# Second norm of a language-model tower: the variance computed one sequence ahead, the values kept by VectorE, one whole tanh two sequences behind, and the next turn between the halves of the second product

## The reference, cut to what matters

```python
h = h + _L0_ffn_ref(_layernorm(h, axis=-1), ...)
h = h + _L1_attn_ref(_layernorm(h, axis=-1), ...)

def _layernorm(x, axis=-1, eps=1e-05):
    m = jnp.mean(x, axis=axis, keepdims=True)
    v = jnp.var(x, axis=axis, keepdims=True)
    return (x - m) / jnp.sqrt(v + eps)

def _L1_attn_ref(x, Wk1, bk1, Wk2, bk2, Wq1, bq1, Wq2, bq2, Wv, bv, ln_w, ln_b, Wo, bo):
    def encode(W1, b1, W2, b2):
        h = jax.nn.gelu(x @ W1 + b1, approximate=False)
        return jnp.tanh(h @ W2 + b2)
    key_phase = encode(Wk1, bk1, Wk2, bk2) * freq * jnp.pi
    query_phase = encode(Wq1, bq1, Wq2, bq2) * freq * jnp.pi
    key_phasor = jnp.cos(key_phase) + 1j * jnp.sin(key_phase)
    V = (x @ Wv + bv).astype(jnp.complex64)
    ...
```

## Time and profile before

| | |
|---|---|
| median of 3 runs | 1166.69 us (1165.56 to 1167.3) |
| profiled execution, its own time | 1167.59 us |
| its span | 1165.8 us |
| busy share of the span | TensorE 95%, VectorE 60%, ScalarE 68%, GpSimd 12% |
| chain that ended last, by engine | TensorE 85%, VectorE 6%, ScalarE 4%, GpSimd 2% |
| the stage of the change | about 872 to 930 us |

### The profile page before, as it was taken

How to read it: one execution, slowest core, us unless ns; L and a number is a source line. 1 busy time by engine, 2 the same in 40 slices (tenths; PEclk the granted TensorE clock), 3 DMA queues, 4 the chain that set the end, 5 groups by cost and what they waited for, 6 DMA issues and landing times.

```text
span 1165.8 us, 62466 instructions
## 1 busy us (share of the span) xinstructions
PE 1103.2 (95%) x26872; PEld 931.7 (80%) x26872; DVE 694.8 (60%) x3130; ACT 795.1 (68%) x4592; POOL 143.2 (12%) x220
## 2 busy tenths in 40 slices
PE   3799999999999999999999999999898699899998
PEld 2699999999999999999999999999544388622322
DVE  7565455555555555555555554444466669899985
ACT  1467677777777777777777777666568888556654
POOL 4200000000000000000000000000104212412110
PEclk9555555555555555555555555555699989999999
DMA  4000000000000000000000000000000000447675
GB/s 142 8 9 9 9 14 9 10 9 9 10 13 9 9 9 10 14 9 9 10 4 4 5 5 4 4 4 4 2 1 1 1 1 1 148 157 291 210 267 173
DMA packets 30545, 47.20 MB, mean 40 GB/s; under 512 B 12274, under 2 KB 21563, under 8 KB 30268
## 3 DMA queue, kind: packets, MB, share of 16 engines
q1 hardware_dynamic: 30268, 43.21, 11.0%
HBM read 40.84 MB, written 2.36 MB: 37 GB/s over the span
## 4 chain that ended last, share of the span: by engine, by line
PE 85%; DVE 6%; ACT 4%; POOL 2%; issue 1%; DMA 1%; SPq 1%; DVEq 0%; ACTq 0%; POOLq 0%
PE bank L657 44%; PE bank L753 7%; PE bank L1383 6%; PE bank L1676 5%; PE bank L736 5%; PE bank L427 4%; PE bank L526 3%; PE bank L731 2%; PE bank L748 1%; PE bank L1581 1%; PE bank L412 1%; POOL stat L1024 1%; PE bank L1416 1%; PE bank L447 1%; DMA bsum<-in_bov 1%
## 5 line engine op out<-in xcount | busy, mean ns | idle before, releaser
L657 PE MATMUL bank<-space,whh_hi 128*128 128x8 f16 x16384 | 609.9, 169 | 7.4 <-DVE space L784 4.2
L657 PEld LDWEIGHTS bank<-space,whh_hi 128*128 128x128 f16 x16384 | 528.7, 105 | 25.5 <-DVE space L784 7.4
L784 DVE TENSOR_TENSOR space<-h_f,space 128x16 f16<-128x16 f32 x2048 | 290.6, 175 | 381.5 <-ACT h_f L765 379.9
L765 ACT ACTIVATE h_f<-bank 128x16 f32<-128x16 f32 x2048 | 300.0, 184 | 230.0 <-PE bank L657 222.5
L771 ACT ACTIVATE space<-bank 128x16 f16<-128x16 f32 x2048 | 299.0, 184 | 1.1 <-PE bank L657 1.1
L657 PE MATMUL bank<-space,whh_lo 128*128 128x32 f16 (+1 forms) x2096 | 145.0, 190 | 0.0
L753 PE MATMUL bank<-space,wih_hi 128*128 128x32 f16 x2048 | 137.1, 188 | 0.0
L427 PE MATMUL bank<-onehot,tab 128*128 128x128 f16 x448 | 116.7, 266 | 0.5 <-DVE prepare_cur L477 0.5
L736 PE MATMUL bank<-xr,wih_hi 128*128 128x32 f16 x512 | 109.8, 214 | 0.0
L1266 ACT ACTIVATE gel<-bank,ebias 128x1024 f32<-128x1024 f32 x64 | 71.3, 1114 | 56.1 <-PE bank L1383 50.6
L731 PE MATMUL bank<-ones,bias 128*128 128x32 bf16 x512 | 102.8, 201 | 0.0
(11 more groups left out here) (288 smaller groups left out, 1559.4 us busy)
## 6 DMA issues: line engine op xcount, KB each, us to landing
space<-weights_kept SPq DMA_DIRECT2D x64, 512.0 KB, 7.9
space<-in_x SPq DMA_DIRECT2D x28, 129.0 KB, 3.1
out<-res SPq DMA_DIRECT2D x8, 256.0 KB, 9.7
space<-in_wrec SPq DMA_DIRECT2D x1, 768.0 KB, 4.0
space<-in_wx SPq DMA_DIRECT2D x1, 740.5 KB, 8.8
brec<-in_brec SPq DMA_DIRECT2D x1, 260.0 KB
ew<-in_ew SPq DMA_DIRECT2D x1, 256.0 KB, 4.1
weights_kept<-wturned SPq DMA_DIRECT2D x8, 32.0 KB, 1.8
```

The source lines that it names most:

```text
L657: mm = pe.matmul(own[:, m, :], w[:, k, m * P:(m + 1) * P], steps(h, k), start=False, stop=False, skip_group_check=True)
L765: act.activation(h_f[layer][:, s % 2, :, :], own, ACT.Tanh, scale=scale[layer]).then_inc(s_h[layer], 1)
L784: dve.tensor_tensor(h[layer][:, :, s % RINGS[layer], 1, :], h_f[layer][:, s % 2, :, :], h[layer][:, :, s % RINGS[layer], 0, :], ALU.subtra ...
```

## The change

The variance of sequence b+1 is computed before the normalising product of b, with its own three columns of `stat` for even and odd sequences (`rstd_row`). The values are kept by VectorE (`values_kept`, one sequence behind) instead of ScalarE. The tanh is one instruction over 1024 columns, runs two sequences behind, and its product goes to banks 2 and 3 or 6 and 7 in turn (`phase_bank`). The second product is split: its first half, the turn of the next sequence, its second half. The last sequence is turned and copied whole. A wait for all tanhs stands before the bias product in bank 6.

The hunk that only removes the semaphores `s_half` and `s_half_kept` is left out.

```diff
@@ -914,6 +913,8 @@
         FF_B1, KQ_B1, KQ_B2, LN_W, LN_B, QUARTER, WR_B, GRID, FF_B2, TURN, BACK = 0, 2, 3, 4, 5, 6, 7, 8, 9, 10, 11
         column = lambda i: col[:, i:i + 1]
         span = lambda b: bass.ds(b * TT, TT)
+        rstd_row = lambda b, i: stat[:, ((2, 3, 4), (0, 1, 5))[b % 2][i], :]
+        phase_bank = lambda b: banks[1 + b % 2 * 2]
 
         block = ctx.enter_context(nc.Block())
 
@@ -1020,8 +1021,8 @@
             def second_rstd(b):
 
                 pool.wait_ge(s_var, b + 1)
-                link(pool.tensor_scalar(stat[:, 3, :], stat[:, 2, :], EPS, None, ALU.add))
-                pool.tensor_tensor(stat[:, 4, :], stat[:, 3, :], nhalf[:, :], ALU.pow).then_inc(s_rstd, 1)
+                link(pool.tensor_scalar(rstd_row(b, 1), rstd_row(b, 0), EPS, None, ALU.add))
+                pool.tensor_tensor(rstd_row(b, 2), rstd_row(b, 1), nhalf[:, :], ALU.pow).then_inc(s_rstd, 1)
 
             for b in range(B):
                 second_rstd(b)
@@ -1120,12 +1121,6 @@
             def second_copy(b):
                 norm_copy(act, xt[:, b * T:(b + 1) * T], bank[5], b)
 
-            def last_copy():
-                for half, (turned, kept) in enumerate(((s_half, s_half_kept), (s_tr, s_xt))):
-                    act.wait_ge(turned, 1 if half == 0 else OPEN + B)
-                    at = (B - 1) * T + half * 512
-                    act.activation(xt[:, at:at + 512], bank[5 + half].bitcast(F16)[:, 0:512], ACT.Copy).then_inc(kept, 1)
-
             def phase_gelu(b):
                 for half in range(2):
                     act.wait_ge(s_kq, b * 2 + half + 1)
@@ -1134,16 +1129,10 @@
                     act.activation(gel[:, half, 0, :], bank[half][:, :], ACT.Gelu, bias=column(KQ_B1),
                                    scale=unscale[S_KQ1]).then_inc(s_kqg, 1)
 
-            def phase_values(b):
-                act.wait_ge(s_v, b + 1)
-                act.activation(vv[:, span(b), :], tokens(bank[4][:, :]), ACT.Identity,
-                               scale=unscale[S_V]).then_inc(s_vr, 1)
-
             def phase_tanh(b):
-                for half in range(2):
-                    act.wait_ge(s_ph, b * 2 + half + 1)
-                    act.activation(rph[:, b * T + half * 512:b * T + half * 512 + 512], bank[2 + half][:, :], ACT.Tanh,
-                                   bias=column(KQ_B2)).then_inc(s_th, 1)
+                act.wait_ge(s_ph, b * 2 + 2)
+                act.activation(rph[:, b * T:(b + 1) * T], phase_bank(b)[:, :], ACT.Tanh,
+                               bias=column(KQ_B2)).then_inc(s_th, 2)
 
             halves_scalar(act, done, SUBS, xt_by[:, :, T - UNIT:T], (bank[5], bank[6]), SUBS, lambda: ff_gelu(0, 0))
             ff_gelu(0, 1)
@@ -1178,22 +1167,17 @@
             second_copy(0)
             ff_kept(B - 1)
             second_high(1)
-            for b in range(B):
-                if 1 < b < B - 1:
-                    second_square(b + 1)
-                if b:
-                    phase_gelu(b - 1)
-                    if b > 1:
-                        second_high(b)
-                    phase_values(b - 1)
-                    phase_tanh(b - 1)
-                    if b < B - 1:
-                        second_copy(b)
-                    else:
-                        last_copy()
+            for b in range(1, B):
+                phase_gelu(b - 1)
+                if b > 1:
+                    second_high(b)
+                    phase_tanh(b - 2)
+                second_copy(b)
+                if b + 2 < B:
+                    second_square(b + 2)
             phase_gelu(B - 1)
+            phase_tanh(B - 2)
             phase_tanh(B - 1)
-            phase_values(B - 1)
             table(ACT.Sin)
 
             def key_cosines(b):
@@ -1456,10 +1440,7 @@
 
             def kq_hidden(b):
                 for half in range(2):
-                    if b == B - 1 and half == 0:
-                        pe.wait_ge(s_half_kept, 1)
-                    else:
-                        pe.wait_ge(s_xt, OPEN + b + 1)
+                    pe.wait_ge(s_xt, OPEN + b + 1)
                     if b:
                         pe.wait_ge(s_kqg, b * 2 + half - 1)
                     on_norm(bank[half][:, :], W_KQ1, P, b, half).then_inc(s_kq, 1)
@@ -1469,12 +1450,12 @@
                     pe.wait_ge(s_vr, b)
                 on_norm_tokens(bank[4], W_V, D, b, B_V).then_inc(s_v, 1)
 
-            def kq_second(b):
-                for half in range(2):
-                    pe.wait_ge(s_kqg, b * 2 + half + 1)
-                    if b:
-                        pe.wait_ge(s_th, b * 2 + half - 1)
-                    pe.matmul(bank[2 + half][:, :], wkq2[:, :], gel[:, half, 0, :], start=True, stop=True).then_inc(s_ph, 1)
+            def kq_second(b, half):
+                pe.wait_ge(s_kqg, b * 2 + half + 1)
+                if b > 1:
+                    pe.wait_ge(s_th, b * 2 - 2)
+                pe.matmul(phase_bank(b)[:, half * 512:(half + 1) * 512], wkq2[:, :], gel[:, half, 0, :], start=True,
+                          stop=True, skip_group_check=True).then_inc(s_ph, 1)
 
             pe.wait_ge(s_big, 1)
             for m in range(KH):
@@ -1531,28 +1512,15 @@
                 digit_at(b, prepared)
                 ff_turned(b)
                 digit_at(b, turned)
-            def last_turn():
-                pe.wait_ge(s_xs, OPEN + B)
-                pe.wait_ge(s_xt, OPEN + B - 1)
-                for half, signal in enumerate((s_half, s_tr)):
-                    for t in range(4):
-                        mm = pe.transpose(bank[5 + half].bitcast(F16)[:, t * P:(t + 1) * P],
-                                          xs[:, half * 4 + t, :, :].rearrange("p a d -> p (a d)"), eye16[:, :])
-                    mm.then_inc(signal, 1)
-
             for b in range(B):
                 kq_hidden(b)
-                if b == B - 1:
-                    kq_second(b)
+                if b < B - 1:
                     kq_values(b)
-                else:
-                    kq_values(b)
-                    kq_second(b)
-                if b + 2 < B:
+                kq_second(b, 0)
+                if 0 < b + 1 < B:
                     second_turn(b + 1)
-                elif b + 1 < B:
-                    last_turn()
-
+                kq_second(b, 1)
+            kq_values(B - 1)
 
             pe.wait_ge(s_vr, B)
 
@@ -1626,6 +1594,7 @@
                 mm.then_inc(s_wo, 1)
 
             pe.wait_ge(s_lnb, 1)
+            pe.wait_ge(s_th, 2 * B)
             pe.matmul(bank[6][:, D:2 * D], ones[:, :], bias[:, B_O:B_O + D], start=True, stop=False, skip_group_check=True)
             pe.matmul(bank[6][:, D:2 * D], lnb[0:D, :], wobd[0:D, 0:D], start=False, stop=True,
                       skip_group_check=True).then_inc(s_row_b, 1)
@@ -1887,11 +1856,13 @@
 
             def second_variance(b):
                 dve.wait_ge(s_sq, b + 1)
-                dve.reduce_sum(stat[:, 2, :], sq[:, :, :], AX.X).then_inc(s_var, 1)
+                dve.reduce_sum(rstd_row(b, 0), sq[:, :, :], AX.X).then_inc(s_var, 1)
 
             def second_out(b):
                 dve.wait_ge(s_rstd, b + 1)
-                dve.tensor_tensor(nrm[:, :, :], xc2[:, b % 2, :, 0:D], spread(stat[:, 4, :]), ALU.mult).then_inc(s_nrm, 1)
+                if b:
+                    dve.wait_ge(s_xs, OPEN + b)
+                dve.tensor_tensor(nrm[:, :, :], xc2[:, b % 2, :, 0:D], spread(rstd_row(b, 2)), ALU.mult).then_inc(s_nrm, 1)
                 dve.wait_ge(s_nrm, b + 1)
                 dve.tensor_tensor(res[:, span(b), :], xc2[:, b % 2, :, :], nrmw[:, :, :], ALU.add)
                 norm_low(dve, b)
@@ -1903,14 +1874,23 @@
                 dve.tensor_tensor(own, own, whole[:, :], ALU.subtract).then_inc(s_thr_r, 1)
 
             dve.wait_ge(s_fcb, 1)
+            def values_kept(b):
+                dve.wait_ge(s_v, b + 1)
+                dve.tensor_scalar(vv[:, span(b), :], tokens(bank[4][:, :]), inv[:, S_V:S_V + 1], None,
+                                  ALU.mult).then_inc(s_vr, 1)
+
             second_in(0)
             second_variance(0)
+            second_in(1)
             for b in range(B):
                 if b + 1 < B:
-                    second_in(b + 1)
+                    second_variance(b + 1)
                 second_out(b)
-                if b + 1 < B:
-                    second_variance(b + 1)
+                if b + 2 < B:
+                    second_in(b + 2)
+                if b:
+                    values_kept(b - 1)
+            values_kept(B - 1)
 
 
             def absolute(b):

```

More of the change, by code:

```diff
@@ L190, in build @@
                              "keys_copied", "memory_added", "memory_summed", "attention_summed", "attention_kept"))
-        s_half, s_half_kept = sem("last_half_turned"), sem("last_half_kept")
         s_row_b, s_row_k, s_bvc = sem("norm_row_spread"), sem("norm_row_kept"), sem("value_bias_centred")
```

## The result

| | before | the change |
|---|---|---|
| median | 1166.72 us (12 runs, 1165.41 to 1168.43) | 1164.7 us (12 runs, 1162.83 to 1166.24) |
| ratio, 95% interval | | 0.9982 [0.9974, 0.999] |
| profiled execution | 1167.59 us, span 1165.8 | 1165.89 us, span 1164.1 |
| first copy c(0) to c(1) | 6.86 us | 5.87 us |
| one turn (between c(3) and c(6)) | 5.57 us | 4.96 us |

The medians are 2.0 us apart, 0.17%. The forecast was 1.2 us; 1164.7 lies in the range and, by less than 2.3 us, among the times that count as no change. The interval of the ratio leaves out 1, so these runs do show a small gain. The rows of the table are of one profiled execution each, and in both of these TensorE's clock stood at half around 885 us.

The account below looks back on a forecast made before the run. The prediction took a 5.57 us ring of VectorE and GpSimd's power to bound the stage. Gains of 0.9 us (start) and 2.2 (turns), less 1.9 (end), made 1.2 us: median 1165.5 us, range 1163.5 to 1168.4.

Parts of the forecast that it names:

- c(0): Start of ScalarE's copy of sequence 0 into `xt`, the first copy; at 883.55 us before.
- c(1): Start of ScalarE's copy of sequence 1 into `xt`; forecast about 889.5 us instead of 890.41.
- the times that count as no change: Times within about 0.2%, or 2.3 us, of the kernel before (1164.4 to 1169.0 us); chance 0.65.
- the ring: Chain of waits per turn before: VectorE's variance, GpSimd's power (2.08 us), product, sum, low part, next variance; closes in 5.57 us.
- Turns of 5.06 us: Steady turns from copy to copy, 5.06 us instead of 5.57, by rings through gelus (5.05) and square (5.06); 2.2 us gained.
- rival 1: VectorE, with 0.16 us of slack, becomes the ring: turns of 5.3 us give 1166.9 us, of 5.57 give 1168.6; chance 0.17.
- Start 0.9 us earlier: Start of the stage: the turn needs only half the second product, so sequence 1's copy starts 0.9 us earlier.
- End 1.9 us longer: Last copy to first cosine: 8.9 us instead of 6.99, as sequence 0's rounding queues behind VectorE's wait for the last values.
- The sum: First cosine of the attention at 928.8 us instead of 929.96, 1.2 us earlier: 0.9 start, 2.2 turns, 1.9 given back.
- rival 2: GpSimd's power holds up VectorE's low part by up to 2.08 us a turn: time 1178 us; chance 0.06.
- rival 4: The end isn't exposed: sequence 7's values are kept in time, ScalarE's table load ends last; 1.5 us better, 1164.0; chance 0.05.
- rival 3: TensorE's half clock behind its pause ends 1 to 2 us sooner (1163.5 to 1164.5, 0.14) or later (1166.5 to 1167.5, 0.10).

Follow-up runs that it names:

- e2: The change with only VectorE's variance put back behind the low part of the same turn: 1166.94 us, 1.0001 [0.9992, 1.0011].
- e3: The kernel before with only the variance computed a sequence ahead: 1165.47 us, 0.9987 [0.9977, 0.9996].
- e1: The change with rounding and absolute value of sequence 0 moved on VectorE ahead of the last values: 1162.34 us, 0.9965 [0.9951, 0.9978].
- e4: The change with the values back on ScalarE, the last ones behind the last tanh: 1163.25 us, 0.9973 [0.996, 0.9985].
- e6: The change with GpSimd's power done a second time in each sequence, into a column nobody reads: 1166.49 us, one run.
- e5: The change with the next sequence's turn behind both halves of the second product: 1166.85 us, 0.9999 [0.999, 1.0009].
- e10: The change with the tanh in halves and one sequence behind again: 1179.21 us, one run.
- e7: The change with 16 unread products in TensorE's pause ahead of the first transposes of the keys: 1163.68 us, 0.9977 [0.9967, 0.9987].
- a0_change_again: The changed kernel unaltered, run and profiled again: 1163.49 us, 0.9982 [0.9973, 0.9991] against the kernel before.
- e8: e4 with 12 unread products ahead of the first transposes of the keys and 5 behind the first turn: 1162.88 us, 0.9971 [0.996, 0.9982].
- e9: e1 with the last tanh in two halves again: 1162.95 us, 0.9968 [0.9956, 0.998].

## Why the prediction was right, point by point

- **GpSimd leaves the ring.** Right, and shown from both sides: e2 puts it back, e3 moves it alone.
- **Turns of 5.06 us.** Measured 4.96. The step that was off is the 2.16 us "from the high part over low part and turn to the next copy": in the earlier trace rows the copy at 901.01 stood behind ScalarE's own tanhs (899.87, two in 1.26 us), while the turn had started at 900.26 and would have let it go at 900.92, by the 0.66 us from turn to copy in the change. Freed of them it takes 2.07 us, which gives 4.97. The six turns took 2.81 us less instead of 2.2, the 0.6 us that the forecast missed.
- **VectorE as a ring.** It idles for 0.28 us a turn (the variance's wait for the square), so rival 1 didn't come about. The values take 0.74 us, more than the 0.70 assumed, but they stand where VectorE would wait anyway.
- **Start 0.9 us earlier.** c(0) to c(1) was forecast as 889.5 less 883.85, 5.65, and is 5.87 with the half clock and 4.32 without. The forecast had taken the half clock of the kernel before as given; the second profile of the change is without it.
- **End 1.9 us longer.** Right: 8.86 against 8.9. e1 shows that 1.5 of it is the rounding behind the last values (7.33 is left, 0.34 above the 6.99 of before), and e4 that the values on VectorE were not needed.
- **The sum.** In the two profiles with the half clock at the start, the change gains 1.93 us from the first copy to the cosine, less 0.22 by which the first copy comes later behind the square of sequence 1 (878.02 to 883.55 before, 877.45 to 883.20 now): 1.7, where the forecast was 1.2. The spans differ by 1.7 us too, but that is partly luck. The stage itself begins 0.57 us earlier (the square of sequence 0 at 874.16 against 874.73), before anything that the change moved; 0.86 us are gained from the first to the third cosine; the dip near 1004 us costs 1.31, and 0.13 more are lost behind it. The same holds for the medians, 2.0 us apart over executions with and without such dips.
- **GpSimd's lock (rival 2)** fell with e6. **The end not exposed (rival 4)** fell with e1.
- **The clock (rival 3)** came about in part, on the side "sooner". TensorE's pause is now 4.55 us instead of 3.49, as forecast. In both profiles of the change the full clock is back 7.9 and 8.4 us behind the first cosine, in both of the kernel before 9.7; and the third cosine follows the first by 14.47 and 14.71 us, against 15.33 and 15.32. That it belongs to the change isn't shown: variants with the same pause (e2, e5, e6, e10) have 13.61 to 15.02, and e1 has 15.34. Fills didn't get the scores of sequence 0 out of the half clock.

## What to carry to other kernels

When a wait leaves a ring, work out the next ring from rows in which the step in question was really waiting for the thing that you keep: a step that also stood behind its own engine's queue gives too long a figure. And ask the chain of waits as well as the timeline: a row of two merged instructions can hide that the second waited for another engine, as the tanhs of e3 did. At the end of a software pipeline read what is queued behind the last stage on the engine that got new work; here three lines in another order (e1) brought the first cosine 1.5 us forward, where the whole change brought it 1.9. An instruction moved off an engine that closes no longer ring than the others buys nothing in the steady part and can cost at the end.

## What the runs showed that was not expected

- TensorE's clock fell in spite of full work shortly before: in e7 it was busy from 924.62 to 928.25, idle for 1.0 us, busy for 1.09, idle for 1.33, and stood at 0.50 in 932 to 934 us. With that work ahead the clock stayed full through the first pause and not through the second.
- GpSimd's power on 128x8 elements takes 1.67 us with VectorE idle and 2.0 to 2.1 beside VectorE's sums and products, its addition 0.24 and up to 0.62. In e2 this brings the last product 0.79 us sooner behind its variance.
- The dip near 1004 us comes and goes between executions of the same or nearly the same program: none in `a0_change_again`, in both profiles of the kernel before, in e1, e2, e3, e4 and e7; there in the change, in e5, e6, e8, e9 and, with all else later, in e10.
- The best median of the study is `e1_round_first`, 1162.34 us, 0.9965 [0.9951, 0.9978] of the kernel before; e9 has the shortest stage (40.93 us). Their intervals, and those of e4 and e8, overlap, so which of them is best isn't settled.
